# Counting degrees with signs on ScalarE, and an experts loop written out

## The reference, cut to what matters

```python
deg = jax.ops.segment_sum(ones, col, num_segments=n_nodes)
dis = jnp.where(deg > 0, deg ** (-0.5), 0.0)
```

```python
gate_scores = x @ Wg + bg
_, idx = jax.lax.top_k(gate_scores, K)
mask = jax.nn.one_hot(idx, E, dtype=x.dtype).sum(axis=-2)
h = jax.nn.gelu(jnp.einsum('td,edh->teh', xf, W1) + b1[None], approximate=False)
y = jnp.einsum('teh,ehd->ted', h, W2) + b2[None]
out = jnp.einsum('ted,te->td', y, mf)
```

## Time and profile before

| | |
|---|---|
| median of 3 runs | 3987.52 us (3983.09 to 3999.14) |
| the profiled execution | 3995.47 us, its span 3993.8 us |
| TensorE busy | 3001.1 us (75%) |
| VectorE busy | 2507.3 us (63%) |
| ScalarE busy | 1234.1 us (31%) |
| GpSimd busy | 1520.8 us (38%) |
| degree count | 55.3 to 259.8 us |
| experts | 1982 to 2431 us |

### The profile page before, as it was taken

One profiled execution on the slowest core, in us unless ns is written; L12 is line 12 of the kernel. 1 busy time (PEld: TensorE's weight loads), 2 busy tenths in 40 slices (PEclk: granted clock), 3 DMA queues, 4 the chain that ended last, 5 costly groups with the idle time before them and its releaser, 6 DMA issues. The chain is left out here.

```text
span 3993.8 us, 66661 instructions
## 1 busy us (share of the span) xinstructions
PE 3001.1 (75%) x21022; PEld 2143.5 (54%) x21023; DVE 2507.3 (63%) x7596; ACT 1234.1 (31%) x2727; POOL 1520.8 (38%) x1558
## 2 busy tenths in 40 slices
PE   2542688886988888748488883169999996988898
PEld 1440455553574545437477772147776774666454
DVE  6966787874343433367844446689887771887544
ACT  1202122331331111013233331255554441343654
POOL 1010677763007777611022224755554452333000
PEclk9655698998998989868599996579999997898999
DMA  4113444443025554445222223843332234111000
GB/s 140 70 36 116 120 144 146 153 150 118 0 95 164 160 160 145 130 153 166 70 64 63 63 63 121 258 134 101 99 99 81 81 88 156 37 37 41 26 22 28
DMA packets 230707, 409.26 MB, mean 102 GB/s; under 512 B 32388, under 2 KB 173111, under 8 KB 225241
## 3 DMA queue, kind: packets, MB, share of 16 engines
q0 software_dynamic: 66816, 182.15, 15.9%
q1 hardware_dynamic: 149056, 168.61, 12.6%
q10 hardware_dynamic: 14620, 55.77, 3.8%
HBM read 306.62 MB, written 99.78 MB: 102 GB/s over the span
## 5 line engine op out<-in xcount | busy, mean ns | idle before, releaser
L1131 POOL DMA_INDIRECT scr<-xn_table,src_i x392 | 373.4, 953 | 340.2 <-PE psum L976 222.6
L1131 POOL DMA_INDIRECT scr<-h_table,src_i x392 | 371.8, 948 | 327.0 <-issue 324.8
L1131 POOL DMA_INDIRECT xnT<-xn_table,src_i x392 | 375.4, 958 | 256.8 <-issue 221.7
L976 PE MATMUL psum<-scr 128*128 128x128 f16 (+1 forms) x3136 | 321.3, 261 | 85.5 <-issue 77.1
L976 PEld LDWEIGHTS psum<-scr 128*128 128x128 f16 (+1 forms) x3136 | 300.0, 154 | 128.3 <-issue 97.6
L758 ACT ACTIVATE scr<-scr,agg 128x128 f16<-128x128 f16 x710 | 253.5, 395 | 78.3 <-DVE scr L741 71.5
L2726 PE MATMUL psum<-scr,xnT 128*128 128x128 f16 x2544 | 202.1, 236 | 65.1 <-issue 60.3
L2635 POOL DMA_INDIRECT scr<-xn_table,scr x106 | 100.2, 945 | 390.8 <-PE psum L2712 325.0
L983 DVE SCALAR_TENSOR_TENSOR agg<-psum,agg 128x256 f32 (+1 forms) x196 | 95.4, 487 | 235.0 <-PE psum L970 216.1
L739 DVE TENSOR_SCALAR scr<-iota,agg 128x128 f16<-128x128 bf16 x710 | 228.3, 326 | 9.4 <-PEq L3014 8.9
L2726 PEld LDWEIGHTS psum<-scr,xnT 128*128 x2544 | 180.0, 104 | 83.5 <-issue 69.7
(11 more groups left out here) (492 smaller groups left out, 6952.2 us busy)
## 6 DMA issues: line engine op xcount, KB each, us to landing
adjacency_table<-agg ACTq DMA_DIRECT2D x13, 1568.0 KB, 6.4
scr<-adjacency_table ACTq DMA_DIRECT2D x13, 1568.0 KB, 7.5
expert_results<-scr SPq DMA_DIRECT2D x106, 128.0 KB, 1.7
scr<-xnT_table SPq DMA_DIRECT2D x98, 128.0 KB
xnT<-xnT_table SPq DMA_DIRECT2D x2, 5376.0 KB, 22.5
agg<-in_L_ffn_W SPq DMA_DIRECT2D x16, 512.0 KB, 9.8
x_table<-scr SPq DMA_DIRECT2D x14, 512.0 KB, 3.1
xn_table<-scr SPq DMA_DIRECT2D x14, 512.0 KB, 4.5
```

Source lines behind the costliest of these rows:

```text
L976: last = pe.matmul(bank[b][:, s, :], lhs, hot[:, hot_b, t, :], start=(t == 0 and n == 0), stop=(t == CT - 1 and n == pieces - 1))
L1131: g.indirect_dma_start(out=rows[:, u, t, :], out_offset=None, in_=table, in_offset=bass.IndirectOffsetOnAxis(ap=index(t), axis=0)).then_in ...
```

## The change

In count_degrees the last 6 (BTS) of a block's 14 columns get no one-hot of their low part. ScalarE makes a stair for each instead: Sign(number - 0.5 - low) over 129 numbers, six activations a block with a bias from SBUF, into `stairs`. TensorE multiplies these with `tiles` into a second PSUM region, `differences`, of 49 x 129. list_edges takes the difference of neighbouring columns, halves it, adds it to the counts of the other eight columns, and writes the sum back to where later phases read it. The numbers 0 to 129 (`upward`) are made by an iota of GpSimd's; VectorE takes 0.5 off them and makes the negated low parts (`minus_low`) before its first block, and ScalarE waits for both. The stairs' places in ScalarE's stream are fixed: two blocks before the root, three after it, three after the copy of the normalized rows, and only then the copies out of PSUM.

In experts the register loop goes. All 106 tiles are written out, the waits count with constants, and each of TensorE, VectorE and ScalarE loads the experts' numbers in four groups: 27, 27, 27 and 25 values. TensorE's and ScalarE's groups stand ahead of tiles 0, 27, 54 and 81, VectorE's two tiles later, ahead of y_rows of the same tiles.

```diff
@@ count_degrees
+BTS = 6
-    tiles, places = part.take([2, BT, NT], BF16), part.take([2, BT, P], BF16)
+    tiles, places = part.take([2, BT, NT], BF16), part.take([2, BT - BTS, P], BF16)
+    stairs, upward, minus_low = part.take([2, BTS, P + 2], BF16), part.take([P + 2]), part.take([ET])
-    counts = c.psum[0:NT, 7, 0:P]
+    counts, differences = c.psum[0:NT, 7, 0:P], c.psum[0:NT, 7, P:2 * P + 1]
-        for out, dst, width in ((tiles, c.dst_high, NT), (places, c.dst_low, P)):
+        for out, dst, width, count in ((tiles, c.dst_high, NT, BT), (places, c.dst_low, P, BT - BTS)):
+        def stair_blocks(a, s, n):
+
+            a.wait_ge(used, s * BLOCKS + n)
+            for t in range(BTS):
+                last = a.activation(stairs[:, n % 2, t, 0:P + 1], upward[:, 0:P + 1], ACT.Sign,
+                                    bias=minus_low[:, ds((s * BLOCKS + n) * BT + BT - BTS + t, 1)])
+            last.then_inc(steps_made, 1)
         @block.vector
         def _(v):
+            v.wait_ge(stair_ready, 1)
+            v.tensor_scalar(upward, upward, 0.5, None, ALU.subtract).then_inc(stair_ready, 1)
+            v.tensor_scalar(minus_low, c.dst_low, -1.0, None, ALU.mult).then_inc(stair_ready, 1)
         @block.scalar
         def _(a):
+            a.wait_ge(stair_ready, 3)
+
             def step(s):
+                stair_blocks(a, s, 0)
+                stair_blocks(a, s, 1)
                 a.wait_ge(vec, s * PER + 3)
                 a.activation(rstd, rstd, ACT.Sqrt).then_inc(root, 1)
+                for n in range(2, 5):
+                    stair_blocks(a, s, n)
                 a.wait_ge(vec, s * PER + PER)
                 a.activation(c.x_all[:, ds(s * TS, TS), :], xn, ACT.Copy)
+                for n in range(5, BLOCKS):
+                    stair_blocks(a, s, n)
                 a.wait_ge(turned, s + 1)
@@ TensorE
-                    for t in range(BT):
-                        last = pe.matmul(counts, tiles[:, n % 2, t, :], places[:, n % 2, t, :], start=False, stop=False,
-                                         skip_group_check=True)
+                    for t in range(BT - BTS):
+                        pe.matmul(counts, tiles[:, n % 2, t, :], places[:, n % 2, t, :], start=False, stop=False,
+                                  skip_group_check=True)
+                    pe.wait_ge(steps_made, s * BLOCKS + n + 1)
+                    for t in range(BTS):
+                        last = pe.matmul(differences, tiles[:, n % 2, BT - BTS + t, :], stairs[:, n % 2, t, 0:P + 1],
+                                         start=False, stop=False, skip_group_check=True)
@@ GpSimd
+            g.iota(upward, pattern=[[1, P + 2]], base=0, channel_multiplier=0, allow_small_or_imprecise_dtypes=True
+                   ).then_inc(stair_ready, 1)
@@ list_edges
-            step.done(v.tensor_copy(counts, c.psum[0:NT, 7, 0:P]))
+            v.tensor_copy(stair_sums, c.psum[0:NT, 7, P:2 * P + 1]).then_inc(stair_steps, 1)
+            v.wait_ge(stair_steps, 1)
+            v.tensor_tensor(stair_counts, stair_sums[:, 1:P + 1], stair_sums[:, 0:P], ALU.subtract).then_inc(stair_steps, 1)
+            v.wait_ge(stair_steps, 2)
+            step.done(v.scalar_tensor_tensor(counts, stair_counts, 0.5, c.psum[0:NT, 7, 0:P], ALU.mult, ALU.add))
+            step.wait()
+            v.tensor_copy(c.psum[0:NT, 7, 0:P], counts)
@@ experts
+    AT_ONCE = 27
+
+    def experts_of(engine, tile):
+
+        n = min(AT_ONCE, MT - tile)
+        _, regs = nc.values_load_multi_w_load_instructions(c.tile_expert[0:1, tile:tile + n], engines=[engine.engine],
-            turns(a, body, 0, 2)
+            for i in range(MT):
+                if i % AT_ONCE == 0:
+                    e = experts_of(a, i)
+                gelu(i, i % 2, i < 2, e[i % AT_ONCE])
+                if i + 2 < MT:
+                    x_high_part(i + 2, i % 2)
-            turns(v, body, 2, 2)
+            for i in range(MT + 2):
+                if i >= 2:
+                    if (i - 2) % AT_ONCE == 0:
+                        e = experts_of(v, i - 2)
+                    y_rows(i - 2, i % 2, i // 2 - 1, e[(i - 2) % AT_ONCE])
+                if i < MT:
+                    g_split(i, i % 2, i < 2)
+                if i + 2 < MT:
+                    x_split(i + 2, i % 2)
-            turns(pe, body, 2, 4)
+            e = []
+            for i in range(MT + 2):
+                if i < MT:
+                    if i % AT_ONCE == 0:
+                        e = e[-2:] + experts_of(pe, i)
+                    hidden(i, i % 2, i < 2, e[i % AT_ONCE - min(AT_ONCE, MT - i // AT_ONCE * AT_ONCE)])
+                if i >= 2:
+                    n = min(i, MT - 1) // AT_ONCE * AT_ONCE
+                    result(i - 2, i % 2, i // 2 - 1, e[i - 2 - min(n + AT_ONCE, MT)])
+                if i + 2 < MT:
+                    turn_x(i + 2, i % 2, i // 2 + 1)
```

More of the change, by code:

```diff
@@ L1200, in count_degrees @@
     hot, used = c.sem("count_onehots"), c.sem("onehots_used")
+    stair_ready, steps_made = c.sem("count_stairs_ready"), c.sem("count_stairs_made")
     vec, root, turned, copied = c.sem("norm1_vec"), c.sem("norm1_root"), c.sem("norm1_turned"), c.sem("norm1_copied")
@@ L1203, in count_degrees @@
     MIDDLE = NS // 2
-    counts = c.psum[0:NT, 7, 0:P]
+    counts, differences = c.psum[0:NT, 7, 0:P], c.psum[0:NT, 7, P:2 * P + 1]
     def onehots(v, s, n):
         v.wait_ge(used, s * BLOCKS + n)
-        for out, dst, width in ((tiles, c.dst_high, NT), (places, c.dst_low, P)):
-            last = v.tensor_tensor(out[:, n % 2, :, :], c.iota16[:, 0:width].unsqueeze(1).broadcast_to([P, BT, width]),
-                                   dst[:, ds((s * BLOCKS + n) * BT, BT)].unsqueeze(2).broadcast_to([P, BT, width]),
+        for out, dst, width, count in ((tiles, c.dst_high, NT, BT), (places, c.dst_low, P, BT - BTS)):
+            last = v.tensor_tensor(out[:, n % 2, :, :], c.iota16[:, 0:width].unsqueeze(1).broadcast_to([P, count, width]),
+                                   dst[:, ds((s * BLOCKS + n) * BT, count)].unsqueeze(2).broadcast_to([P, count, width]),
                                    ALU.is_equal)
@@ L1268, in _ @@
         def _(pe):
+            pe.matmul(differences, c.zeros[:, 0:NT], c.zeros[:, 0:1].broadcast_to([P, P + 1]), start=True, stop=False,
+                      skip_group_check=True)
             pe.matmul(counts, c.zeros[:, 0:NT], c.zeros[:], start=True, stop=False, skip_group_check=True
@@ L1332, in list_edges @@
     counts, countsT, node = part.take([P])[0:NT, :], part.take([NT]), part.take([NT])
+    stair_sums, stair_counts = part.take([P + 1])[0:NT, :], part.take([P])[0:NT, :]
+    stair_steps = c.sem("stair_steps")
     pairs = []
@@ L2594, in experts @@
     PARTS = ((0, 0), (0, 1), (1, 0))
-    def experts_of(engine, tile, n):
-        _, regs = nc.values_load_multi_w_load_instructions(c.tile_expert[0:1, ds(tile, n)], engines=[engine.engine],
+    AT_ONCE = 27
+    def experts_of(engine, tile):
+        n = min(AT_ONCE, MT - tile)
+        _, regs = nc.values_load_multi_w_load_instructions(c.tile_expert[0:1, tile:tile + n], engines=[engine.engine],
                                                            min_val=0, max_val=EXPERTS - 1)
         return list(regs)
[L2602 to L2613, removed]
     with nc.Block() as block:
@@ L2692, in _ @@
             x_split(1, 1)
[L2694 to L2701, removed]
-            turns(v, body, 2, 2)
-            e = experts_of(v, MT - 2, 2)
-            for b in range(2):
-                y_rows(MT - 2 + b, b, MT // 2 - 1, e[b])
+            for i in range(MT + 2):
[7 more added lines that the diff above has]
+                    x_split(i + 2, i % 2)
         @block.tensor
@@ L2745, in _ @@
             turn_x(1, 1, 0)
[L2747 to L2754, removed]
-            turns(pe, body, 2, 4)
-            e = experts_of(pe, MT - 2, 2)
-            for b in range(2):
-                result(MT - 2 + b, b, MT // 2 - 1, e[b])
+            e = []
[9 more added lines that the diff above has]
+                    turn_x(i + 2, i % 2, i // 2 + 1)
     c.constants.end(16)
```

1 line of the change is left out of this document (added).

## The result

The changed kernel takes 3975.89 us (median, 3964.36 to 3991.86) against 3995.62 us of the kernel before, measured beside it: a ratio of 0.9952, 95% interval 0.9937 to 0.9967. On the 3987.5 us of the forecast that is 19 us gained, or 3968. The forecast was 58 us, and its range ended at 3962: the direction was right, the size was not. The profiled execution took 3971.5 us, its span 3969.8.

What follows compares the result with a forecast made beforehand. VectorE was taken to bound the degree count and TensorE the experts. Count -23 us and experts -35 us sum to -58, so 3930 us against 3987.5; the range for 8 in 10 is 3900 to 3962.

Steps and rivals of the forecast that it cites:

- the limit for an ACTIVATE: Degree count: ScalarE's added stairs cost nothing until they pass VectorE's time, put at 0.34 us an ACTIVATE.
- The late start thus costs 1.8 us, not 9.6: Count's start: VectorE waits for the new iota, but the old kernel lost time there too; bounds 0.5 and 6 us.
- Rival (c): Count: Sign is not in Sqrt's table, so table loads put ScalarE ahead; +10 us, 3940 us; 4 in 100.
- the sign that was named against it: Count: if the forecast is right, no ACT table load beyond three appears in the phase.
- -85.5: Experts: removing 17 loop turns' holes gains 81 us, and about 4.5 more at the end.
- TensorE's groups, 35: Experts: TensorE's four register load groups, 4 x 1.2 + 106 x 0.286 = 35 us added, wholly exposed.
- VectorE's groups, 22: Experts: VectorE's groups take 8.6 us each, about 5.5 exposed, four times: 22 us added.
- The lower clock, 8: Experts: after each of eight holes a hidden stage runs at the lower clock; 1 us each, 8 us added.
- Per tile, 14: Experts: constant wait thresholds save TensorE's sequencer 0.13 us a tile, 14 us gained; bounds 0 and 0.44.
- Rival (a): Experts: loads only change places, VectorE's and ScalarE's groups fully exposed, constants bring nothing; 3990 us, no change; 4 in 100.
- its half: Experts: half of rival (a)'s effect, giving 3955 to 3975 us; 8 in 100.
- Rival (d): Experts: written-out tiles' instructions arrive slower than they are used; 4015 us at 0.8 us a tile; 4 in 100.

Runs made afterwards that it cites:

- count_alone: The kernel before with only the degree count's part of the change (new count and list, old experts' loop): 3969.93 us, ratio 0.994.

## Why the prediction was wrong, step by step

**The count's steps stood.** First comparison: 65.3 predicted, 64.25 measured. Seven normalizing operations of step 0 ending at 78.5: at 78.2. The wait between steps 2 and 3: 5.7, and 5.3 measured. A step of 22.36 us: the later ones came 21.7 apart (184.50 and 206.22, their BATCH_NORM_STATS2). TensorE late before block 7 by 1.3: waits of 0.5 to 1.7 us, 1.0 on average. The last PSUM copies ended at 228.7 us (231.2), and the list began 5.9 us after them (4.4) in this trace, 4.5 in count_alone. So the list's start, 234.5 for 235.6, is nearer than its two parts, and that is luck. The list lost 0.96 (1.1). By its own terms the limit for an ACTIVATE comes to 0.36 us, not the 0.34 given; nothing hung on it.

**One step of it was wrong in its reason.** "The late start thus costs 1.8 us, not 9.6": moving the start sooner gave 9.4. The step compared with the old kernel, whose normalization had been stretched by GpSimd's iotas, and took that loss for one that any kernel pays. With shorter blocks VectorE passes that place before the long iotas begin. The forecast of the total wasn't harmed, since both ends were timed right; the advice that would follow from it (the place of the iota matters little) was.

**Rival (c), Sign and Sqrt in different tables, did not come,** though the sign that was named against it, no table load beyond three, did not hold. In steps 0 to 2 there are two loads a step (6 in all, at 64.60, 69.54, 90.04 and so on), in steps 3 to 6 none, though Sign and Sqrt alternate there just the same (0.21 us between the Sqrt at 211.23 and the next Sign). So one table holds both. Steps 0 to 2 are one register loop and 3 to 6 another; the first has the two loads in its body, the second has none. Their 6 x 1.28 = 7.7 us lie beside VectorE's work, which waited 0.2 us for the root in the whole phase. The six activations of a block took 1.8 us as taken from the earlier trace rows. The Trainium skill (ScalarE: Activation LUTs, What ACT_TABLE_LOAD costs) puts a switch at 2.66 us with a drain of 1.38; here the load at 64.60 lasted 1.28 and the first Sign began at 65.89, so no drain is seen behind it.

**The experts: four terms, of which two are the error.** The sum was -85.5 + 35 + 22 + 8 - 14 = -35, and 6 came out.
- *TensorE's groups, 35.* This is the first step that failed. The term 4 x 1.2 for the TENSOR_LOADs measured 2.37 + 6.6 + 6.6 + 6.1 = 21.7: 17 us over. The term of 106 x 0.286 was right to the microsecond.
- *VectorE's groups, 22.* This is the second, by the same price: the load in a group was put at 1.0 us and took 2.3 once and 5.8 to 6.3 three times. The second group took 13.3 us and not 8.6, and TensorE's waits for VectorE were 5.3, 11.2, 10.8 and 10.2 us, where 5.5 was put for each. The pitch of those tiles was 5.5, 12.6, 10.9 and 11.6 us over a steady one: 41 us, 19 over. The overlap was nearly right: TensorE had 13.3 - 11.2 = 2.1 us of work beside the group, 3.1 in the sum (8.6 - 5.5).
- *The lower clock, 8.* The tiles behind the holes made up nearly all: 4 us, 4 better.
- *Per tile, 14.* The steady pitch fell from 3.34 to 3.26 us, not to 3.21: 8.5 gained, 5.5 over. Of the two ends (0 and 0.44 us a tile) the value was rightly near the low one.

17 + 19 - 4 + 5.5 = 37 against the 41 that are missing; 4 us I can't assign. In the total the later phases add their own: the untouched sum of the second layer was 8.6 us shorter in the profiled execution after than before, the second norm 4.3 longer.

**What failed was the reading of one row.** The earlier trace rows gives the old TENSOR_LOADs as 551/674/2193 ns. I took 1.2 us, between the median and the longest, and applied it to loads of 27 values, three times the size, without asking what makes loads of one size four times as long as others. The row had two populations, and they took turns (0.6 and 2.1 us). Scaled by the number of values, the median gives 2.3 us for 27 and the longest 2.19 x 27/8 = 7.4; both were in the trace, and the second was no rival of mine. The Trainium skill (Runtime: NRT & Kernel Launch, Instruction fetch mechanics) has a price near it, about 200 ns a register for a TENSOR_LOAD; it speaks of registers loaded from HBM, and the loads here are from SBUF. The trace comes near it where a load begins off a 16-byte boundary (6606/27 = 245 ns), and not where it begins on one (2371/27 = 88 ns, 1625/24 = 68).

**Rival (a)** had the time and not the mechanism. The measured ratio gives 3968 us, within the 3955 to 3975 of its half, to which I gave 8 in 100. But the rival took VectorE's and ScalarE's groups as fully exposed at 8.6 us each and the constants as worth nothing. ScalarE's cost nothing, 2.1 us of VectorE's were covered, and the constants brought 8.5. That the number fits is luck. The forecast's own range has a flaw as well: its terms give 3987.5 - 21 - 15 = 3951.5 for the upper end, and no term is named for the other 10 us up to 3962.

**Rival (d)** is refuted: written-out tiles came 3.26 us apart for 3.34 in the loop, and with cheap loads and no check the same written-out tiles took 365.5 us for the loop's 401.7.

## What to carry to other kernels

When values are loaded into registers in a group, begin each group at a multiple of 16 bytes, put the engines' groups beside each other in time, and ask what the work for each value is: here a bounds check, 30 us of TensorE. How far the lesson of the multiple of 16 bytes reaches is shown here for int32 values in SBUF only. A row whose shortest and longest differ fourfold at one shape holds two kinds, and an estimate must say which kind the new instructions are, and scale it by their size. And a loss that the old kernel has at a place isn't a floor under the new one: ask whether the new timing still meets it.

## What the runs showed of the hardware that was not expected

- A TENSOR_LOAD of int32 values from SBUF took 2.37 us for 27 values from a multiple of 16 bytes and 6.60 us from other places, on TensorE. All its loads here fit 0.1 us and 0.24 for each access, if an access is 16 bytes from a multiple of 16 and one value from elsewhere. From elsewhere VectorE took 6.3 us and ScalarE 6.0 (0.23 and 0.22 a value). The accesses are inferred from such sizes and places, not seen.
- The bounds check of a loaded value was 0.286 us of TensorE's sequencer and 0.28 of VectorE's.
- VectorE's seven operations of 256 floats took 2.35 us alone, 3.10 beside GpSimd's iotas of up to 60 numbers, 4.56 beside those of 62 and 160, and 9.62 beside those of up to 260.
- A phase without an edit varied by 19 us of 340 between kernels (granted clock 0.85 to 0.88), more than the 6 that the experts' half moved.
